# Selective scan: ScalarE's, TensorE's and POOL's units re-placed among a group's 32 steps

## The reference, cut to what matters

```
u, z = split(x0 @ in_proj_w.T)                 # x0 = rmsnorm(x); u and z are 512 wide
u = silu(causal_conv(u, conv_w, 4 taps) + conv_b)
dt, B, C = split(u @ x_proj_w.T)
dt = softplus(dt @ dt_proj_w.T + dt_proj_b)
s = s * exp(dt * A) + (dt * u) * B_t           # a state of 16 for each of 512 channels, token by token
y = sum_n(s_n * C_n) + u * D_skip
x1 = (y * silu(z)) @ out_proj_w.T + x
x  = x1 + mlp(rmsnorm(x1))                     # 256 -> 512 -> 512 -> 256, relu
```

## Time and profile before

| what | value |
| --- | --- |
| median of 3 runs | 2609.38 us (2602.1 to 2622.14) |
| profiled execution | 2626.54 us, span 2624.8 us |
| mean granted TensorE clock | 0.915 |
| first and last scan start | 45.2 and 1032.8 us |
| busy shares of the span | PE 88%, DVE 73%, ACT 58%, POOL 51% |

### The profile page before, as it was taken

How to read it: one execution, slowest core, us unless ns; L and a number is a source line. 1 busy time by engine, 2 the same in 40 slices (tenths; PEclk the granted TensorE clock), 3 DMA queues, 4 the chain that set the end, 5 groups by cost and what they waited for, 6 DMA issues and landing times. The chain is left out here.

```text
span 2624.8 us, 48915 instructions
## 1 busy us (share of the span) xinstructions
PE 2320.2 (88%) x17037; PEld 1626.2 (62%) x17037; DVE 1907.8 (73%) x4315; ACT 1511.8 (58%) x3369; POOL 1327.8 (51%) x1271
## 2 busy tenths in 40 slices
PE   5869899999999988889999979888986998999797
PEld 2555656565656566567777746556663776777655
DVE  5998989898999997166766557777756555566545
ACT  6768787877878774333333334445444666765522
POOL 2796969696968785143233224444444232331411
PEclk7969998999999988899999979999867999898798
DMA  6545444444444443110000243332202000000300
GB/s 204 163 137 159 127 150 139 145 155 133 155 127 157 125 149 93 28 50 1 1 1 1 35 92 61 69 66 52 50 2 75 16 22 18 18 22 18 110 15 9
DMA packets 139462, 206.74 MB, mean 79 GB/s; under 512 B 24482, under 2 KB 59427, under 8 KB 139091
## 3 DMA queue, kind: packets, MB, share of 16 engines
q1 hardware_dynamic: 137234, 200.73, 26.8%
q0 software_dynamic: 960, 2.62, 0.3%
q10 hardware_dynamic: 1024, 0.26, 0.1%
HBM read 161.29 MB, written 14.68 MB: 67 GB/s over the span
## 5 line engine op out<-in xcount | busy, mean ns | idle before, releaser
L427 POOL TENSOR_TENSOR ma_seen<-ma_state,ma_cs 128x1024 f32<-128x1024 f32 x256 | 601.9, 2361 | 215.9 <-DVE ma_state L1071 207.7
L1071 DVE TENSOR_TENSOR_SCAN ma_state<-ma_decay,ma_last,ma_drive 128x512 f32<-128x512 f32 x512 | 630.0, 1265 | 19.8 <-ACT ma_decay L916 16.0
L1058 DVE TENSOR_TENSOR ma_drive<-ma_weight,ma_bs 128x512 f32<-128x512 f32 x512 | 325.8, 682 | 27.2 <-ACT ma_weight L903 27.2
L916 ACT ACTIVATE ma_decay<-ma_dt,ma_a_neg 128x512 f32<-128x512 f32 x512 | 338.7, 710 | 0.7 <-DVE ma_dt L1135 0.6
L647 PEld LDWEIGHTS ma_acc<-ident,ma_seen 128*128 128x128 f32 x2048 | 254.4, 151 | 132.3 <-issue 65.5
L647 PE MATMUL ma_acc<-ident,ma_seen 128*128 128x128 f32 x2048 | 286.8, 291 | 46.3 <-POOL ma_seen L427 46.2
L2138 ACT ACTIVATE sw_prob<-sw_turned 128x512 f32<-128x512 f32 (+1 forms) x256 | 135.5, 581 | 194.2 <-PE sw_turned L2028 176.8
L2200 DVE CUSTOM_DVE_ANT_0 sw_score<-sw_score,both_band 128x256 f32<-128x256 f32 (+1 forms) x512 | 197.6, 448 | 67.2 <-PE sw_score L2014 56.2
L104 POOL TENSOR_TENSOR moe_h_low<-both_V,light_wqkv 128x512 fp32r<-128x512 f32 x80 | 104.9, 1311 | 247.5 <-DVE light_wqkv L100 240.1
L1936 POOL TENSOR_SCALAR_AFFINE_SELECT sw_prob<-sw_prob 128x512 f32<-128x512 f32 x128 | 83.9, 655 | 230.1 <-ACT sw_prob L2138 230.1
L1660 DVE TENSOR_TENSOR both_V<-both_V,moe_up 128x512 f32<-128x512 f32 x80 | 55.0, 688 | 120.6 <-PE moe_up L1449 75.4
(11 more groups left out here) (591 smaller groups left out, 5777.6 us busy)
## 6 DMA issues: line engine op xcount, KB each, us to landing
ma_bs<-bc_rows SPq DMA_DIRECT2D x256, 256.0 KB, 3.3
ma_cs<-bc_rows SPq DMA_DIRECT2D x256, 256.0 KB, 3.3
ma_h<-kept_taps SPq DMA_DIRECT2D x28, 256.0 KB, 6.0
both_wide<-both_kh SPq DMA_DIRECT2D x28, 192.0 KB, 4.6
both_wide<-both_qh SPq DMA_DIRECT2D x20, 256.0 KB, 4.6
...
```

Source lines behind the costliest of these rows:

```text
L427: g.tensor_tensor(out=seen[n % RR][:, :, :], in0=state[n % SR][:, :, :], in1=each(cs[n % CR][:, :], 2), op=ALU.mult).then_inc(S["seen_full ...
L916: a.activation(decay[s % DR][:, :], dt[:, m, :], ACT.Exp, scale=a_neg[:, m, k:k + 1]).then_inc(S["decay_done"], 1)
L1058: v.tensor_tensor(out=drive[mm][:, :], in0=weight[mm][:, :], in1=bs[n % CR][:, :], op=ALU.mult).then_inc(S["drive_done"], 1)
L1071: v.tensor_tensor_scan(state[n % SR][:, mm, :], decay[s % DR][:, :], drive[mm][:, :], last[:, k, m:m + 1], ALU.mult, ALU.add).then_inc(S[" ...
```

## The change

No instruction is added, removed or altered, and the code before the first and after the last group is as it was. What changes is the q at which units stand, and on ScalarE also whether a unit stands ahead of a step's `keeps` and `decays` or behind them. Ahead of the decays now stand, on ScalarE: `squares1` and `outputs(0)` (slot 2), `turned_back(3)` (4), `mixed(0)` (6), `gates_out(1)` (9), `halos` (11), `projected(0)` (12), `outputs(2)` (19), `rows_out` (21), `hidden2(0)` (27), `hidden2(2)` and `normalized` (31). `moves(i, 1)` goes from slot 15 to slot 14. On VectorE the gate of half 0 goes from step 18 to step 20, and two of the statistics move by a scan or two. On POOL `root("2")` and `adds` go from 10 to 11, `dt_rest` from 24 to 25, `dt_sum` from 27 to 26, and `finishes` from 29 to 27, ahead of `dt_weight`. TensorE's units `back`, `mix`, `gates`, `hidden2` stand earlier and closer together.

```
@@ -194,34 +194,88 @@
-    if q in (3, 4, 5) and one:
-        found += [("back", i - 1, j) for j in ((0,), (1, 2), (3,))[q - 3]]
-    if q in (5, 6, 7, 8) and one:
-        found.append(("mix", i - 1, q - 5))
-    if q in (7, 8, 9, 10):
-        found.append(("gates", i, q - 7))
...
+    if q == 13 and front:
+        found.append(("project", i + 1, 2))
+    if q == 13 and front:
+        found.append(("conv", i + 1, 0))
+    if q == 14 and front:
+        found.append(("project", i + 1, 3))
+    if q == 14 and front:
+        found.append(("conv", i + 1, 1))
+    if q == 16 and front:
+        found.append(("conv", i + 1, 2))
+    if q == 16 and front:
+        found.append(("conv", i + 1, 3))
+    if q == 18 and two:
+        found.append(("out", i - 2, 2))
+    if q == 18 and one:
+        found.append(("turn2", i - 1, 0))
+    if q == 20 and one:
+        found.append(("turn2", i - 1, 1))
     if q == 20 and front:
         found.append(("rows", i + 1, 0))
...
@@ -483,24 +537,23 @@
-                    if q == 10 and one:
+                    if q == 11 and one:
                         root("2", ss2, rstd2, i - 1)
                         adds(i - 1)
+                    if q == 25 and front:
+                        dt_rest(i + 1, 0)
+                    if q == 26 and front:
+                        dt_log(i + 1, 0)
+                        dt_sum(i + 1, 0)
+                    if q == 27 and two:
+                        finishes(i - 2)
+                    if q == 28 and front:
+                        dt_weight(i + 1, 0)
...
@@ -919,14 +972,39 @@
+                    if q == 12 and front:
+                        projected(i + 1, 0)
+                    if q == 14:
                         moves(i, 1)
-                    if q == Q - 1 and front:
-                        moves(i + 1, 0)
                     if q == 17:
                         gates(i)
+                    if q == 19 and two:
+                        outputs(i - 2, 2)
+                    if q == 21 and front:
+                        rows_out(i + 1)
+                    if q == 27 and one:
+                        hidden2(i - 1, 0)
+                    if q == 31 and front:
+                        moves(i + 1, 0)
                     if n + 2 < Q * GROUPS:
                         decays(n + 2)
...
@@ -1112,13 +1198,19 @@
-                        if (q, mm) == (18, 0):
+                        if (q, mm) == (20, 0):
                             gate(i, 0)
```

More of the change, by code:

```diff
@@ L209, in step_units @@
-    if q in (11, 12, 13, 14) and front:
-        found.append(("project", i + 1, q - 11))
-    if q in (13, 15, 16, 17) and front:
-        found.append(("conv", i + 1, (13, 15, 16, 17).index(q)))
-    if q == 19 and one:
-        found += [("turn2", i - 1, k) for k in range(DH)]
+    if q == 0:
+        found.append(("steps", i, 2))
+    if q == 1:
+        found.append(("steps", i, 3))
+    if q == 1 and two:
+        found.append(("out", i - 2, 0))
+    if q == 2 and two:
+        found.append(("out", i - 2, 1))
@@ new lines, in step_units @@
+    if q == 2 and one:
+        found.append(("back", i - 1, 0))
+    if q == 2 and one:
+        found.append(("back", i - 1, 1))
+    if q == 2 and one:
+        found.append(("back", i - 1, 2))
+    if q == 3 and one:
+        found.append(("back", i - 1, 3))
+    if q == 3 and one:
+        found.append(("mix", i - 1, 0))
+    if q == 4 and one:
+        found.append(("mix", i - 1, 1))
+    if q == 6 and one:
+        found.append(("mix", i - 1, 2))
+    if q == 6 and one:
+        found.append(("mix", i - 1, 3))
@@ L215, in step_units @@
+    if q == 20 and one:
+        found.append(("turn2", i - 1, 1))
     if q == 20 and front:
         found.append(("rows", i + 1, 0))
-    if q == 22 and front:
-        found += [("steps", i + 1, m) for m in range(2)]
-    if q in (21, 22, 23, 24) and one:
-        found.append(("hidden1", i - 1, q - 21))
+    if q == 21 and one:
+        found.append(("hidden1", i - 1, 0))
     if q == 21 and two:
         found.append(("out", i - 2, 3))
-    if q in (26, 27, 28, 30) and one:
-        found.append(("hidden2", i - 1, (26, 27, 28, 30).index(q)))
+    if q == 22 and front:
+        found.append(("steps", i + 1, 0))
@@ new lines, in step_units @@
+    if q == 22 and front:
+        found.append(("steps", i + 1, 1))
+    if q == 22 and one:
+        found.append(("hidden1", i - 1, 1))
+    if q == 23 and one:
+        found.append(("hidden1", i - 1, 2))
+    if q == 24 and one:
+        found.append(("hidden1", i - 1, 3))
+    if q == 27 and one:
+        found.append(("hidden2", i - 1, 0))
+    if q == 28 and one:
+        found.append(("hidden2", i - 1, 1))
+    if q == 28 and one:
+        found.append(("hidden2", i - 1, 2))
+    if q == 29 and one:
+        found.append(("hidden2", i - 1, 3))
@@ L936, in body @@
                         steps_exp(i, 1)
-                    if q == 2 and front:
-                        squares1(i + 1)
+                    if q == 2 and two:
+                        outputs(i - 2, 1)
+                    if q == 2 and one:
+                        turned_back(i - 1, 0)
+                        turned_back(i - 1, 1)
+                        turned_back(i - 1, 2)
                     if q == 3:
@@ L942, in body @@
                         scaled1(i + 1)
[L943 to L953 removed]
+                    if q == 7 and one:
+                        mixed(i - 1, 1)
+                        mixed(i - 1, 2)
@@ L987, in body @@
-                    if q in (27, 28, 29, 31) and one:
-                        hidden2(i - 1, (27, 28, 29, 31).index(q))
-                    if q == Q - 1 and two:
-                        for j in range(GT):
-                            normalized(i - 2, j)
+                    if q == 29 and one:
+                        hidden2(i - 1, 1)
+                    if q == 31 and one:
+                        hidden2(i - 1, 3)
             squares1(0)
```

121 lines of the change are left out of this document (73 added, 48 removed).

## The result

The changed kernel takes 2587.08 us (median of 6 runs, 2582.41 to 2599.43) against 2607.38 us of the kernel before on the same chip (6 runs): a ratio of 0.9904, 95% interval 0.9874 to 0.9934. The ratio is taken over all runs; the medians lie 20.3 us apart, 0.8%, where 39 us were forecast. The profiled execution took 2585.69 us with a span of 2584.0 us; its mean granted TensorE clock is 0.929.

A forecast was written before the change was run, and what follows sets the result against it. VectorE was taken to set the scan's pace, with TensorE close behind. Of 54.1 us of waits 15.0 would stay (9.6 + 1.2 + 1.2 + 3.0), gaining 39: 2609.4 - 39 = 2570 us, range 2554 to 2604.

The forecast's parts named there:

- The waits at step 16: VectorE's six waits on ScalarE's moves, some 16.4 us, forecast to be gone.
- at the gate: VectorE's gate waits in step 18, 7.1 us in all, forecast to be gone with the gate in step 20.
- at step 0: VectorE's six waits at the next group's first step, 10.8 us; 0.2 us each forecast to stay, 1.2 in all.
- the DMA's: Scans' waits on the DMA of B's row, 3.7 us; 1.2 us forecast as what may stay.
- The chain behind the later gate: Work from step 20's gate to scan 26; waits at 21 and 26 forecast at 1.6 us together, 9.6 in six groups.
- Units ahead of decays: ScalarE units newly placed before decays; forecast cost 0.5 us a group, 3.0 in all.
- Rival 1: TensorE's clock falls at the later gate, losing 10 to 12 us in six groups: 2581; chance 0.16.
- Rival 2: The waits only move, to places with small slack: 2595, range 2583 to 2620; chance 0.27.
- Rival 3: TensorE becomes the bound at a lower clock, making the kernel slower: 2653 at 0.83; chance 0.07.
- Its own signs of being wrong: Decay waits over 20 us, middle-group TensorE clock under 0.93, or scans waiting where units now stand ahead of decays.

The follow-up runs named there:

- x4: Changed kernel with the gate of half 0 back in step 18 instead of 20; median 2600.86 us, ratio 0.9954 to the kernel before.
- x8: Changed kernel with slot 2's units behind the decays, hidden2(3) in slot 30, and turned2(0) and outputs(2) behind decays(21); 2589.51 us, ratio 0.9934.
- x1: Changed kernel with squares1 and outputs(0) of ScalarE's slot 2 back behind its decays; 2596.59 us, ratio 0.9947.
- x7: Changed kernel plus one unused 512-column matmul in each of TensorE's slots 31 and 0, filling its waits for POOL; 2603.11 us, ratio 0.9941.
- x9: Changed kernel with out(3) behind the first steps units on TensorE and ScalarE, VectorE's last statistic from step 24 to 26; 2587.90 us, ratio 0.9917.
- x10: x7 plus three unused matmuls ahead of starts in groups 0 and 1; 2585.99 us, ratio 0.9894 to the kernel before.
- x2: Changed kernel with TensorE's last hidden2 moved from slot 29 back to slot 30; 2583.31 us, ratio 0.9893.
- x3: Changed kernel with POOL's finishes back behind the weight, from step 27 to 29; 2599.45 us, ratio 0.9959.
- x11: x10 with x9's edit added; 2580.26 us, ratio 0.9869 to the kernel before.
- x5: Kernel before with only ScalarE's moves(i, 1) moved from slot 15 to slot 14; 2613.19 us, ratio 1.0012.
- x6: Kernel before with moves(i, 1) in slot 14 and the gate of half 0 in step 20; 2608.03 us, ratio 0.9992.

## Why the prediction was right or wrong

**Direction and main mechanism: right.** VectorE sets the pace, and the change gains by taking waits from between its scans: 54.1 us became 34.8, which is 19.3, and the stretch is 18.3 shorter. The waits at step 16, at the gate and at step 0 and the DMA's are gone as forecast, with 0.7 us at the steps 0 and 1.2 at gates left over (1.2 and none were forecast). The chain behind the later gate was forecast at 1.6 us a group for steps 21 and 26 and took 1.24 + 0.73 = 1.97, with some 0.95 at step 27 in three groups: 13.7 us in place of 9.6. x4, which has no such waits, shows that it is the gate's cost, and x8 that it is one account.

**The size: half of the forecast, and one term above all.** 34.8 us are left over where 15.0 were forecast. The largest part of these 19.8 is one mis-sized term. "Units ahead of decays" stood with 3.0 us, 0.5 a group, out of slack counted from durations at full clock ("1.9 us, of a spare of 2.2"). Measured are 12.1 us at steps 4 to 6. Another 5.2, at step 23 of groups 0 and 1, had no term at all, and the later gate's chain cost 4.1 more than its 9.6. x1 shows that the order in slot 2 isn't the cause at step 4. x7 shows the cause by taking it away, and x9 by having groups with it and groups without it under the same code: the `steps` matmuls and sums ran at 0.50. Against the next gate, ScalarE's second `steps_raw` starts 2.0 us behind it in the changed kernel (540.60 to 538.60) and 0.7 ahead of it in x7 (531.98 to 532.67); the 2.7 us between are the 2.35 and the 0.3 spare.

**Rival 1 was right in kind and wrong in place.** It had the clock fall at the gate in step 20. In the middle groups TensorE waits 1.56 us there and the clock stays at 1.00; in groups 0 and 1, without an `out` ahead of the gate, it waits 4.51 and 3.83 us and the clock falls to 0.50, which costs 5.2 us. With the filling of x10 both are gone; with the same 3.83 us in x7's group 1 the clock held. The falls that count are at the other end of the group, behind two waits of 1.42 and 1.22 us. My argument against it ("the idle is shorter than the work around it") looked at one wait, and not at a stretch where TensorE is left with sums alone. The change itself made that stretch: before, the last `hidden2` ran between the sums of slots 0 and 1 at full clock, and now it is done by slot 30. x2, which puts one back by a slot, halves the time at 0.50 in groups 3 and 4 and moves the fall behind the `steps` in groups 5 and 6. POOL's part is open, since x3 has an idle of its own. The Trainium skill, "TensorE: Matmul & The Clock Gate", section "A second HAM failure mode: psum-queue depth-cycling", has frequent short idles between groups of matmuls make the clock swing between its two levels; 530 to 546 us fit it, with waits of 1.42 and 1.22 us. But x9's group 4, with the same two waits at 1.00, and x9 and x11, with the same 1.02 us and different clocks behind it, show that such waits don't always bring it down. The price that the prediction put on rival 1 was also read too high: rows 7 have TensorE busy for 3.13 of the 4 us at 0.50, which is 1.6 us of work at full clock and not 2.

**Rival 2** ("the waits only move") holds for single edits (x1, x5, x6), for x8, and for group 4 of x7. Of the whole it tells half: 54.1 us of waits fell by 19.3 where 39 were to go, and the new ones stand where rival 2 said, behind units ahead of the decays. It said so of small slacks each met late; the largest of them was met late because of the clock. The measured 2587 lies in its range (2583 to 2620), with a chance of 0.27, and not in the forecast's (2558 to 2578). **Rival 3** fell: a middle group's clock is 0.94 and VectorE is busy 117.16 of 122 us.

**The time.** 2609.4 - 39 = 2570 had the gain wrong by 19 to 20 us. 2587 lies within the range of 2554 to 2604 because that was drawn wide enough to take in two rivals, and by the prediction's own measure, 1%, a change of 0.8% (of 0.96% by the ratio) is one of "within 1%". Its own signs of being wrong came out two against one: waits on decays are 29.0 (over 20), and scans wait at step 4, behind units that now stand ahead of the decays; the clock in a middle group, 0.94, is above 0.93. That the profiled execution before had its surplus in the third layer was not seen; it did no harm, since waits were counted and not spans. That the last group has no wait but those after its scans was read from a window that begins at 927; that group waits 1.71 us at its step 0, at 916.84, which the six waits at step 0 include.

**Left open.** In group 2 of the changed kernel, which has no wait at step 4, the clock is low for about 7 us and not for 10 to 14 as in groups 3 to 7. What makes it fall in one group and not in the next, under the same code and with the same waits ahead, no run settles.
